# Twelve weighted-value steps of an attention group, grouped into six pairs

## The reference

```
x = layernorm(x + attention(x))      # 32 heads of 16, rope, causal softmax, plus a gated prefix of 10 adapter tokens
x = layernorm(x + ffn(x))            # base_w, base_b, and a top-2-of-16 router over low-rank experts (rank 64)
```

```
scores = q @ k.T / 4                 # [1024, 1024], masked above the diagonal
y      = softmax(scores) @ v         # [1024, 16]
```

## Time and profile before

| | |
|---|---|
| median of 3 runs | 876.29 us (875.12 to 880.5) |
| span of the profiled execution | 874.7 us |
| median less that span | 1.6 us |
| busy share of the span: TensorE, VectorE, ScalarE, GpSimd | 98%, 82%, 54%, 27% |
| groups 1 to 14, first score to first score of group 15 | 365.47 us |
| one group of them (group 10) | 26.08 us |

### The profile page before, as it was taken

The page is one execution under the profiler, slowest core; times in us unless marked ns, Lnnn a source line. Parts: engine busy times, 40 slices in busy tenths (PEclk is TensorE's granted clock), DMA queues, the critical chain, the costliest instruction groups (busy, mean ns, idle before and its releaser), DMA issues.

```text
span 874.7 us, 15938 instructions
## 1 busy us (share of the span) xinstructions
PE 855.2 (98%) x5386; PEld 551.8 (63%) x5386; DVE 721.0 (82%) x2228; ACT 470.5 (54%) x1040; POOL 236.7 (27%) x277
## 2 busy tenths in 40 slices
PE   9999999999999999999999999999999999999996
PEld 6788867785444444444444454444468888888885
DVE  4865667779999999999999999995676777777766
ACT  4333313223788888888888888888742121212110
POOL 0222220222222333323333336333332222222221
PEclk9999999999999999999999999999999999999999
DMA  7316180727133331133442253313010010101011
GB/s 271 121 49 193 61 230 24 218 80 182 34 74 75 75 75 42 35 74 75 75 75 47 34 118 75 74 52 101 30 37 25 25 48 24 48 24 48 25 36 37
DMA packets 32402, 66.61 MB, mean 76 GB/s; under 512 B 5772, under 2 KB 7244, under 8 KB 32332
## 3 DMA queue, kind: packets, MB, share of 16 engines
q1 hardware_dynamic: 32332, 65.72, 29.4%
HBM read 44.11 MB, written 20.97 MB: 74 GB/s over the span
## 4 chain that ended last, share of the span: by engine, by line
PE 81%; DVE 8%; issue 3%; ACT 2%; DMA 1%; POOL 1%; SPq 1%; DVEq 0%; POOLq 0%; ACTq 0%
PE bank L1644 16%; PE bank L1512 16%; PE bank L448 11%; PE bank L1520 11%; PE bank L450 10%; PE bank L449 10%; PE bank L1626 2%; PE bank L1457 2%; DVE bank L1070 2%; PE bank L1473 1%; DVE xtl L1195 1%; ACT xth L874 1%; DVE mx L1073 1%; PE bank L1720 1%; DMA ks<-k_parts 1%
## 5 line engine op out<-in xcount | busy, mean ns | idle before, releaser
L920 ACT ACTIVATE pt<-bank 128x512 f32<-128x512 f32 (+3 forms) x768 | 325.8, 496 | 67.9 <-PE bank L1512 61.4
L1070 DVE CUSTOM_DVE_ANT_0 bank<-bank,cmask 128x512 f32<-128x512 f32 (+3 forms) x512 | 234.3, 527 | 9.2 <-PE bank L1520 6.4
L1512 PE MATMUL bank<-qs,ks 50*128 50x512 f32 (+3 forms) x768 | 216.2, 397 | 0.4 <-ACT pt L920 0.2
L1512 PEld LDWEIGHTS bank<-qs,ks 50*128 50x128 f32 x768 | 109.3, 184 | 136.0 <-ACT pt L920 117.6
L1073 DVE TENSOR_REDUCE mx<-bank 128x1 f32<-128x512 f32 x256 | 160.8, 687 | 9.8 <-PE bank L1520 8.4
L1644 PE MATMUL bank<-pt,vb 128*32 128x512 f32 (+3 forms) x1536 | 163.4, 498 | 0.8 <-POOL pt L701 0.8
L1520 PE MATMUL bank<-ks,qs 48*128 48x512 f32 (+3 forms) x768 | 161.2, 385 | 2.8 <-DVE mx L1070 1.3
L701 POOL TENSOR_SCALAR_AFFINE_SELECT pt<-pt 128x512 f32<-128x512 f32 x128 | 81.5, 638 | 284.3 <-ACT pt L920 284.3
L1520 PEld LDWEIGHTS bank<-ks,qs 48*128 48x128 f32 x768 | 90.6, 185 | 33.5 <-DVE mx L1070 11.2
L644 POOL TENSOR_TENSOR part<-rope,part 128x1024 fp32r<-128x1024 f32 x16 | 38.2, 2386 | 165.0 <-ACT part L768 165.0
L874 ACT CAST xth<-bank 128x512 fp32r<-128x512 f32 x15 | 8.8, 586 | 135.0 <-PE bank L1720 135.0
(11 more groups left out here) (196 smaller groups left out, 1441.1 us busy)
## 6 DMA issues: line engine op xcount, KB each, us to landing
qs<-q_parts SPq DMA_DIRECT2D x34, 256.0 KB, 4.0
ks<-k_parts SPq DMA_DIRECT2D x34, 256.0 KB, 6.9
q_parts<-part SPq DMA_DIRECT2D x32, 256.0 KB, 3.4
k_parts<-part SPq DMA_DIRECT2D x32, 256.0 KB, 3.6
qs<-q_parts SPq DMA_DIRECT2D x34, 128.0 KB, 5.0
ks<-k_parts SPq DMA_DIRECT2D x34, 128.0 KB, 5.9
vb<-in_x SPq DMA_DIRECT2D x16, 256.0 KB, 2.7
out<-outb SPq DMA_DIRECT2D x16, 256.0 KB, 2.0
```

The lines of the kernel that those rows point to most:

```text
L920: act.activation(pt[k % PT_BUFS][:, h, 0:width(st)], half(n % SCORE_BUFS)[:, 0:width(st)], ACT.Exp, scale=float(HD) ** -0.5).then_inc(S("e ...
L1070: last = ve.tensor_tensor_reduce(blk, blk, cmask[:, BANK - nk * P:], 1.0, NEG, ALU.add, ALU.max, mx[m][:, 0, h, qt:qt + 1])
L1512: pe.matmul(half(n % SCORE_BUFS)[:, 0:q1 - q0], ks[slot_of(g)][r0:r0 + KX, h // 2, kb * P:(kb + 1) * P], qs[slot_of(g)][r0:r0 + KX, h // 2 ...
```

## The change

The list `VALUES_AT` names the same six late places, each twice. Steps 1, 3, 5, 7, 9 and 11 stay where they were. Steps 0, 2, 4, 6, 8 and 10 move to the place of the step after them. TensorE then does two weighted steps with nothing between. The loop that places them is written so that two steps can have one place. It applies to groups 0 to 14.

```
-VALUES_AT = [13, 17, 19, 22, 26, 33, 37, 42, 44, 48, 51, 57]
+VALUES_AT = [17, 17, 22, 22, 33, 33, 42, 42, 48, 48, 57, 57]
...
-assert all(a < b for a, b in zip(VALUES_AT, VALUES_AT[1:])) and VALUES_AT[-1] - SCORE_BANKS < VALUES_AT[0]
+assert all(a <= b for a, b in zip(VALUES_AT, VALUES_AT[1:])) and VALUES_AT[-1] - SCORE_BANKS < VALUES_AT[0]
...
                     score(g, c)
-                    if g > 0 and c + SCORE_BANKS in values_at(g - 1):
-                        weighted(g - 1, values_at(g - 1).index(c + SCORE_BANKS))
-                    if c in values_at(g):
-                        weighted(g, values_at(g).index(c))
+                    for st in range(NS):
+                        if g > 0 and c + SCORE_BANKS == values_at(g - 1)[st]:
+                            weighted(g - 1, st)
+                    for st in range(NS):
+                        if c == values_at(g)[st]:
+                            weighted(g, st)
```

## The result

The changed kernel takes 972.1 us (median of 4 runs, 959.6 to 975.1) against 877.8 us for the kernel before in the same comparison. The ratio is 1.099, with a 95% interval of 1.091 to 1.107. The forecast was 911 us with a range up to 923, so the direction was right and the size wrong: 87 us more by the ratio (94 by the medians), where 35 had been forecast.

What follows compares the result with a forecast made beforehand. Three score banks leave ScalarE at most three exponentials in store, so longer TensorE pieces idle it. 4.94 - 2.29 - 0.25 = 2.40 us a group, 15 times, less 1 us: 874.7 + 35, plus 1.6, gives 911 us; range 892 to 923.

Steps and rivals of the forecast that it cites:

- The failed step: Whole program: each pair occurs 15 times, at 2.40 us more a group, so 36 us more.
- in the longer waits: Sign of being wrong: TensorE's granted clock falls from its upper level in the longer waits; no size given.
- the term of 1 us: Group 0: ScalarE's gaps don't set its length, so 1 us comes off the program's sum.
- 2.40 us a group: One group: streaming parts added at six pairs, less ScalarE's gaps removed and a fuller store: 4.94 - 2.29 - 0.25 us.
- the 0.25 us taken off: Pairs at chunks 0, 33 and 42: ScalarE could arrive with more in store, 0.25 us together, ends 0 and 0.8.
- the 2.29 us: Removed steps at chunks 13, 19, 26, 37, 44 and 3: ScalarE's gaps there, together 2.29 us, are won.
- 0 to 0.4 us: VectorE, ten banks read from chunk 23 to 33: may finish last, allowed 0 to 0.4 us a group more.
- the account: ScalarE, edit by edit: a pair adds the moved step's streaming part and wins only the gap at its old place.
- the 0.86 us of a 512-wide step: TensorE's weighted step: streaming part for 512 columns is 0.86 us, read as four passes, beside a fixed 0.14 us.
- The first: Rival, faster: TensorE is the bound, each pair saves a passage out of and into scores; 864 us, chance 0.08.
- The third: Rival, slower by half as much: TensorE ends last in chunks 23 to 42, saved passages count; 894 us, chance 0.13.
- The fourth: Rival, worse: VectorE runs dry at pairs, lost time not made up, another 1 us a group; 926 us, chance 0.08.

Runs made afterwards that it cites:

- extra matmuls like those above: Changed kernel plus extra 128-column matmuls (256 at chunk 21) at eight chunks where TensorE waits for an exponential: 936.5 us, ratio 1.064.
- the kernel with two extra matmuls: Changed kernel plus two extra matmuls of 128 columns, at chunks 38 and 39: 968.5 us, ratio 1.099.
- The singles: Six kernels, each the kernel before with one of the change's six steps moved, pairs at 17, 22, 33, 42, 48, 57: ratios 1.004 to 1.064.
- the pair at 48: Kernel before with only step 8 moved, from chunk 44 to 48 (chunk 0 of the next group): 885.9 us, ratio 1.010.
- The pair at 33: Kernel before with only step 4 moved, from chunk 26 to 33: 937.4 us, ratio 1.064.
- The pair at 42: Kernel before with only step 6 moved, from chunk 37 to 42: 917.9 us, ratio 1.047.
- A cheap matmul in the wait: Kernel before with only step 4 moved to chunk 33, plus 128-column matmuls at chunks 28 and 33 of groups 1 to 14: 895.2 us, ratio 1.022.

## Why the prediction was wrong

**The failed step** is the one over the whole program, "15 x 2.40 = 36 us". It takes every microsecond at the clock of the trace before. The text names a fall of the granted clock "in the longer waits" only among the things that would prove it wrong, with no price and no chance. The kernel before gave a hint: in group 0 it already has extra matmuls like those above (`keep_on`, L1531), and the text passes over them. In groups 1 to 14 of the changed kernel's trace 102 us run at the lower level, in group 0 another 27. At full clock a group takes 30.83 - 1.65 = 29.2 us, from a group with one 3.4 us stretch and the price of such a stretch (at most 29.4, by the kernel with two extra matmuls). So of the 84.6 us in groups 1 to 14, 14 x 3.1 = 43 are the pairs' own, and 41 are the clock. Group 0 lost another 11 us; the term of 1 us taken off for it has no run, as no kernel shows its six pairs at full clock. The pairs' own 43 us alone, an estimate, would have made about 920 us, near the upper end of the range.

**A second term was mis-sized.** The forecast had 2.40 us a group, with ends of 1.85 and 3.05; it measured 3.1. The singles show where. Of the 0.25 us taken off for a fuller store at chunks 0, 33 and 42 at most 0.10 were there, at chunk 0 (the pair at 48: 0.42 us where the gaps give 0.52). And the 2.29 us that ScalarE was to win at the removed places aren't all won. The pair at 33 cost 0.87 and not 0.37 us, since VectorE, which works without a pause around these chunks, ends last there; the text allowed 0 to 0.4 us for that and left it out of the sum. The pair at 42 cost 0.73 and not 0.45 us, with a new gap of 0.22 us at chunk 41. All six singles add up to 3.38 us, together they cost 3.1; the difference has no run of its own.

**What held.** ScalarE, not TensorE, is short of work behind a weighted step: its busy time is unchanged, its gaps stand behind the pairs at 0.93 to 1.30 us where 0.9 to 1.3 were forecast (2.08 at the lower clock, 0.99 without it), and four of the six singles follow the account to 0.1 us, including the one that costs nothing. A pair lacks the second fixed part of 0.14 us (1.64 us again). VectorE's idle time rose from 0.8 us in a group to 5.1 in the 30.9 us of group 9; about 3 had been forecast for 28.5 us. One reading in the text is wrong without weight for the sum: the 0.86 us of a 512-wide step are four matmuls recorded as eight, not four passes of one.

**The rivals.** The first, that a passage saved is time saved, would have made every single pair faster; none is. So the Trainium skill's rule on tiling modes, TensorEngine Tiling (Array Packing), section Key Properties, names a cost that the rows agree with but that wasn't on the path. The third, TensorE's saved passages counting between chunks 23 and 42, is not borne out: the pairs at 33 and 42 cost more than the gaps give, not less. The fourth, VectorE running dry at the pairs and its time not made up, has no run of its own; what the singles show of VectorE is the stretch around chunk 28, where it has no pause at all. For what did happen there is a passage in the Trainium skill too, on its page TensorE: Matmul & The Clock Gate, section A second HAM failure mode: psum-queue depth-cycling: frequent short idle times between groups of matmuls make the clock swing between its levels. The traces agree: no printed wait before the fall at 533.3 us, back to the group's first score, was longer than 0.63 us. It speaks against this change and should have been the rival on the slow side.

Open stays which waits bring the fall (a wait hidden in a matmul's modelled end isn't printed) and what sets how long the clock stays down: 3.4 us in eight of 14 groups of the changed kernel, 17 us in six of 14 groups of the kernel with the pair at 33.

## What to carry to other kernels

Where a producer has only as many result banks as it can fill ahead, work inserted on the producer is free up to what the consumer has in store, and costs all of its time beyond that; put such work in single pieces, and read at each place how much store is left and how large the gap behind it is. Price the granted clock as well: in a kernel whose TensorE is nearly always busy, a few new waits of a quarter of a microsecond can cost more through the clock than by their own length. A cheap matmul in the wait tells which of the two it is, and here it gave back 42 us of 56.

## What was not expected of the hardware

TensorE fell to its lower level with no printed wait above 0.63 us, about 1.6 us of them in a group of 30.9 us, and with TensorE busy 18.20 of the 19.5 us before the fall; with the pair at 33 alone a single wait of 0.27 us is printed between the first score of group 2 and its fall, and the stretch there lasted 17 us. The pattern repeats: groups 4 to 6 of the changed kernel take 31.81, 35.64 and 34.27 us, groups 12 to 14 take 31.81, 35.64 and 34.13.
